# Wave attention: weights by tanh, one per head and two heads later, behind a guard on the amplitudes; VectorE takes the second half of the scores for two heads of four

## The reference, cut to what matters

```
FREQS = [31.0, 37.0, 41.0, 43.0, 47.0]
sim = einsum('bhid,bhjd->bhij', q, k) / sqrt(hd) / (abs(temperature)[0] + 0.1)
scores = zeros_like(sim)
for fi, freq in enumerate(FREQS):
    scores = scores + alpha[h, fi] * sin(2 pi * sim / freq + phi[h, fi])
w = sigmoid(scores)
w = w / (sum(w, axis=-1, keepdims=True) + 1e-10)
out = einsum('bhij,bhjd->bhid', w, v)
```

```
'alpha': jax.random.normal(ks[5], (N_HEADS, len(FREQS)), dtype=jnp.float32) * 0.1
...
factors = {'L0_attn_a_Wq': 8.0, 'L0_attn_a_Wk': 8.0, 'L0_attn_a_Wv': 3.655,
 'L0_attn_a_alpha': 8.0, 'L0_attn_a_phi': 8.0,
...
for name, factor in factors.items():
    out[name] = (out[name] * factor).astype(out[name].dtype)
```

## Time and profile before

| what | value |
|---|---|
| median of 3 runs | 3933.75 us (3931.38 to 3935.47) |
| the profiled execution | 3933.19 us, its span 3931.4 us |
| granted TensorE clock over the span | 0.924 |
| busy share of the span: PE, DVE, ACT, POOL | 81%, 75%, 72%, 24% |
| instructions | 70146 |

### The profile page before, as it was taken

How to read it: one execution, slowest core, us unless ns; L and a number is a source line. 1 busy time by engine, 2 the same in 40 slices (tenths; PEclk the granted TensorE clock), 3 DMA queues, 4 the chain that set the end, 5 groups by cost and what they waited for, 6 DMA issues and landing times. The chain is left out here.

```text
span 3931.4 us, 70146 instructions
## 1 busy us (share of the span) xinstructions
PE 3171.9 (81%) x26580; PEld 1974.0 (50%) x26580; DVE 2951.2 (75%) x4169; ACT 2817.8 (72%) x2401; POOL 925.5 (24%) x983
## 2 busy tenths in 40 slices
PE   4788888888888898898638943798998998998890
PEld 2232233223323332233236941688888888887790
DVE  7788888888888888888565545678787878876562
ACT  3999999999999999999604313576776776774330
POOL 2010111011010101110001442544334435330336
PEclk8899999999999999999868977799999999998995
DMA  5877887788788877877521225412213113112122
GB/s 160 306 295 301 301 330 293 303 311 320 299 306 317 309 300 299 333 293 297 220 71 63 62 54 171 68 27 36 47 20 54 27 27 56 26 18 71 33 61 69
DMA packets 311330, 683.35 MB, mean 174 GB/s; under 512 B 155296, under 2 KB 228608, under 8 KB 310560
## 3 DMA queue, kind: packets, MB, share of 16 engines
q1 hardware_dynamic: 302368, 661.87, 48.6%
q0 software_dynamic: 8704, 17.84, 2.0%
HBM read 90.73 MB, written 52.10 MB: 36 GB/s over the span
## 5 line engine op out<-in xcount | busy, mean ns | idle before, releaser
L740 PE MATMUL psA<-wave,diag 128*128 128x512 f32 x2560 | 1174.2, 606 | 117.3 <-DVE score L879 75.0
L801 ACT ACTIVATE wave<-wave 128x2048 f32<-128x2048 int32 x640 | 1184.8, 1904 | 45.6 <-DMA wave<-score 41.5
L740 PEld LDWEIGHTS psA<-wave,diag 128*128 128x128 f32 x2560 | 468.4, 191 | 727.5 <-issue 594.4
L879 DVE SCALAR_TENSOR_TENSOR score<-wave,par,psA 128x1024 f32<-128x1024 f32 x256 | 316.3, 1278 | 290.2 <-PE psA L740 290.2
L678 POOL TENSOR_TENSOR diag<-ident,par 128x128 f32<-128x128 f32 x384 | 142.5, 399 | 1493.5 <-PE psA L740 1493.3
L851 DVE TENSOR_SCALAR score<-s,par 128x2048 int32<-128x2048 int32 x384 | 482.1, 1285 | 9.2 <-DMA wave<-score 6.1
L879 DVE SCALAR_TENSOR_TENSOR score<-wave,par,score 128x1024 f32<-128x1024 f32 x384 | 470.3, 1282 | 0.0
L1785 POOL COPY kb<-ks 48x1024 bf16<-48x1024 bf16 x160 | 320.9, 2005 | 567.3 <-PE psR L1845 380.6
L716 PE MATMUL psO<-score,Vg 128*9 128x512 f32 x1056 | 284.6, 689 | 105.0 <-ACT score L781 105.0
L1935 ACT ACTIVATE W<-psR 128x1024 f32<-128x1024 f32 x256 | 249.4, 1023 | 133.3 <-PE psR L1870 133.2
L1926 ACT COPY r<-psR 128x1024 f32<-128x1024 f32 x256 | 248.6, 1021 | 103.9 <-PE psR L1845 103.9
(11 more groups left out here) (262 smaller groups left out, 4798.0 us busy)
## 6 DMA issues: line engine op xcount, KB each, us to landing
wave<-score SPq DMA_DIRECT2D x384, 1023.9 KB, 6.3
wave<-s SPq DMA_DIRECT2D x128, 1023.9 KB, 5.2
ks<-kb_parts SPq DMA_DIRECT2D x56, 384.0 KB, 6.2
qs<-qb_parts SPq DMA_DIRECT2D x32, 384.0 KB, 6.2
ys<-f_ys SPq DMA_DIRECT2D x36, 256.0 KB
wave_out<-og SPq DMA_DIRECT2D x33, 256.0 KB, 8.2
o<-wave_out SPq DMA_DIRECT2D x8, 1024.0 KB, 5.3
qp<-qa_parts SPq DMA_DIRECT2D x32, 192.0 KB, 7.2
```

What stands on the lines that cost most here:

```text
L740: mm = pe.matmul(psA[:, kt, :], diag[:, h % 2, f, :], wave[:, h % 2, f, kt * L:(kt + 1) * L], start=(f == 0), stop=(f == PE_F - 1 or (h in ...
L801: act.activation(wave[:, h % 2, f, :], angle[:, h % 2, f, :], ACT.Sin, scale=float(TWO_PI / 2.0 ** 32)).then_inc(sine, 1)
L879: return dve.scalar_tensor_tensor(out=score[:, u * HG + h, cols], in0=wave[:, h % 2, f, cols], scalar=par[:, u, 1, h * NF + f:h * NF + f + ...
```

## The change

1. **Guard.** `far` was 1 where `bound` reached FAR x 31 / 8. Now VectorE takes the maximum of `bound` scaled by 8 / (120 x 31) and of all squared amplitudes, and `far` is 1 where that maximum is at least NEAR = 1.0.
2. **Weights.** In the plain branch Tanh takes Sigmoid's place: sigmoid(s) is 0.5 + 0.5 tanh(s / 2). The missing 0.5 times the sum of the values is added when `psO` is taken out: TensorE sums the values over the keys (`psV`, a matmul with one column), VectorE halves that (`half_v`), ScalarE uses it as a bias. Each head's weights are made behind the sines of the head two later (`weigh`), not four heads at once. The general branch keeps Sigmoid, but also one head at a time.
3. **Scores.** For heads 0 and 2 of each group VectorE takes out the second half (`take_scores` on VectorE, between the angles of head n+1 and the sums of head n).
4. GpSimd clears `Vg`, whose rows are now 32 wide for a head; one Silu of one column is the first activation of the block.

The diff, cut to its core:

```diff
+EVAC_HEADS = (0, 2)
+NEAR = 1.0
...
             def values(g, slot, heads):
                 if heads[0] == 0:
                     pe.wait_ge(v_ready, g + 1)
+                    pe.wait_ge(half_ready, g + C_HALF)
+                    for kt in range(QT):
+                        mm = pe.matmul(psV[:], Vg[:, slot ^ 1, kt, :, :].rearrange("p h d -> p (h d)"),
+                                       Vg[:, slot ^ 1, kt, 0, HD:VW], start=(kt == 0), stop=(kt == QT - 1))
+                    mm.then_inc(v_summed, 1)
...
-            def sigmoids(g, slot):
-                for h in range(HG):
-                    act.wait_ge(added, g * HG * ADDS - (HG - 1 - h) * ADDS + C_ADDED)
-                    act.activation(score[:, slot * HG + h, :], score[:, slot * HG + h, :], ACT.Sigmoid)\
-                       .then_inc(weighed, 1)
+            def weigh(m, at, general):
+                act.wait_ge(added, (m + 1) * ADDS + C_ADDED)
+                if general:
+                    act.activation(score[:, at, :], score[:, at, :], ACT.Sigmoid).then_inc(weighed, 1)
+                else:
+                    act.activation(score[:, at, :], score[:, at, :], ACT.Tanh, scale=0.5).then_inc(weighed, 1)
...
                             if f in (2, NF - 1) and more:
                                 tu, th, tg = (u, h + 2, g) if h < HG - 2 else (1 - u, h + 2 - HG, g + 1)
-                                take_scores(n + 2, tu, th, tg, f // 4, general)
-                        if h == 0:
-                            sigmoids(g, 1 - u)
+                                if f == 2 or th not in EVAC_HEADS:
+                                    take_scores(n + 2, tu, th, tg, f // 4, general)
+                        weigh(n - 2, (u * HG + h - 2) % AR, general)
...
+            act.activation(og[:, 0:1], params[:, 0, 0, 0:1], ACT.Silu)
             act.wait_ge(far_ready, 1)
             with act.If(act.value_load(far[0:1, 0:1])):
                 all_heads(True)
...
                         if not final:
                             make_angles(n + 1, nu, nh, ng, general)
+                        tu, th, tg = (u, h + 2, g) if h < HG - 2 else (1 - u, h + 2 - HG, g + 1)
+                        if th in EVAC_HEADS and not (last and u == 1 and h >= HG - 2):
+                            take_scores(n + 2, tu, th, tg, general)
                         add_sines(n, u, h, g)
-
-
-            dve.tensor_scalar(far[:], bound[:], FAR * min(FREQS) / HD, None, ALU.is_ge).then_inc(far_ready, 1)
+                        if h == 2:
+                            halve_values(g, u)
+
+            amps = params[:, :, 1, :]
+            dve.tensor_scalar(reach[:, 0:1], bound[:], HD / (FAR * min(FREQS)), None, ALU.mult).then_inc(reached, 1)
+            dve.tensor_tensor(reach[:, 1:].rearrange("p (a n) -> p a n", a=GPB), amps, amps, ALU.mult
+                              ).then_inc(reached, 1)
+            dve.wait_ge(reached, 2)
+            dve.tensor_reduce(top_reach[:], reach[:], AX.X, ALU.max).then_inc(reached, 1)
+            dve.wait_ge(reached, 3)
+            dve.tensor_scalar(far[:], top_reach[:], NEAR, None, ALU.is_ge).then_inc(far_ready, 1)
```

More of the change, by code:

```diff
@@ L572, in wave_attention @@
         og = sb(c, "og", [P, L])
-        Vg = sb(c, "Vg", [P, 2, QT, HG, VW])
+        Vg = sb(c, "Vg", [P, 2, QT, HG, P // HG])
+        half_v = sb(c, "half_v", [P, 2])
+        reach = sb(c, "reach", [P, 1 + GPB * HG * NF])
+        top_reach = sb(c, "top_reach", [P, 1])
         psS = ps(c, "psS", [P, 2, L])
@@ L576, in wave_attention @@
         psO = ps(c, "psO", [P, L])
+        psV = ps(c, "psV", [P, 1])
         qk_loaded = [sem(c, f"qk_loaded{i}") for i in range(2)]
@@ L776, in take_scores, with outputs @@
                                    scale=float(2 ** FRAC) / FREQS[0]).then_inc(s_ready, 1)
-            def sigmoids(g, slot):
-                for h in range(HG):
-                    act.wait_ge(added, g * HG * ADDS - (HG - 1 - h) * ADDS + C_ADDED)
-                    act.activation(score[:, slot * HG + h, :], score[:, slot * HG + h, :], ACT.Sigmoid)\
-                       .then_inc(weighed, 1)
-            def outputs(g):
+            def weigh(m, at, general):
[4 more added lines that the diff above has]
+                    act.activation(score[:, at, :], score[:, at, :], ACT.Tanh, scale=0.5).then_inc(weighed, 1)
+            def outputs(g, slot, general):
                 act.wait_ge(valued, 2 * g + 2 + C_VALUED)
                 act.wait_ge(out_stored, g * 16 + C_STORED)
-                act.copy(og[:], psO[:]).then_inc(out_taken, 1)
+                if general:
+                    act.copy(og[:], psO[:]).then_inc(out_taken, 1)
+                else:
+                    act.wait_ge(half_ready, g + 1 + C_HALF)
+                    act.activation(og[:], psO[:], ACT.Identity, bias=half_v[:, 1 - slot:2 - slot],
+                                   scale=0.5).then_inc(out_taken, 1)
             def pair(gg, last, general):
@@ L804, in pair @@
                                 tu, th, tg = (u, h + 2, g) if h < HG - 2 else (1 - u, h + 2 - HG, g + 1)
-                                take_scores(n + 2, tu, th, tg, f // 4, general)
-                        if h == 0:
-                            sigmoids(g, 1 - u)
+                                if f == 2 or th not in EVAC_HEADS:
+                                    take_scores(n + 2, tu, th, tg, f // 4, general)
+                        weigh(n - 2, (u * HG + h - 2) % AR, general)
                         if h == HG - 1:
-                            outputs(g)
+                            outputs(g, 1 - u, general)
             def all_heads(general):
                 for h in range(2):
-                    for half in range(2):
-                        take_scores(h, 0, h, 0, half, general)
+                    take_scores(h, 0, h, 0, 0, general)
+                    if h not in EVAC_HEADS:
+                        take_scores(h, 0, h, 0, 1, general)
                 act.wait_ge(cleared, 2)
@@ L818, in all_heads @@
                 pair(NG // 2 - 1, True, general)
-                sigmoids(NG, 1)
-                outputs(NG)
+                for h in (HG - 2, HG - 1):
+                    weigh((NG - 1) * HG + h, HG + h, general)
+                outputs(NG, 1, general)
+            act.activation(og[:, 0:1], params[:, 0, 0, 0:1], ACT.Silu)
             act.wait_ge(far_ready, 1)
@@ L852, in make_turns, with take_scores @@
                                   ALU.mult, ALU.add).then_inc(done, 1)
+            def take_scores(n, u, h, ng, general):
+                cols = slice(HALF, 2 * HALF)
+                dve.wait_ge(s_ps, n * 2 + 2 + C_SPS)
+                if not (isinstance(n, int) and n < 2):
+                    dve.wait_ge(carried[0][h % 2], (ng * (HG // 2) + h // 2) * 16)
+                if general:
+                    dve.tensor_copy(s[:, h % SR, cols], psS[:].rearrange("p a n -> p (a n)")).then_inc(s_ready, 1)
+                else:
+                    dve.wait_ge(par_ready, ng + 1)
+                    dve.tensor_scalar(first[:, h % SR, cols], psS[:].rearrange("p a n -> p (a n)"),
+                                      float(2 ** FRAC) / FREQS[0], par[:, u, 0, h * NF:h * NF + 1],
+                                      ALU.mult, ALU.add).then_inc(s_ready, 1)
             def make_angles(n, u, h, gn, general):
@@ L936, in all_heads @@
                 pair(NG // 2 - 1, True, general)
+                halve_values(NG, 0)
             with dve.If(dve.value_load(far[0:1, 0:1])):
```

27 lines of the change are left out of this document (21 added, 6 removed).

## The result

The changed kernel takes 7365.12 us (median; 7359.96 to 7366.48) against 3932.57 for the kernel before beside it: a ratio of 1.873, 95% interval 1.870 to 1.876. The forecast was 7,355. The profiled execution took 7366.48 us, the longest of the four.

What follows compares the result with a forecast made beforehand. ScalarE bounds the old heads; in the general branch VectorE's angles and the copy wait do. 137.3 us, 127 periods of 40.9 (5194) and 29.5 put the last store at 5361, +3421 on 3933.2: 7,355 us, range 6,960 to 7,610.

Steps and rivals of the forecast that it cites:

- The branch: Guard before the heads: largest amplitude 2.196, square 4.82, exceeds 1.0, so VectorE and ScalarE take the general branch for all heads.
- A frequency: VectorE's angles in the general branch: four dependent instructions of 2048 columns, 6.045 us per frequency, 30.3 us for five.
- The wait for the burst: VectorE's next angles wait for the copy of frequency 2, 10.6 us behind the first issue; idle 3.5 or 2.3 us.
- What was costed at nothing: General branch heads: ScalarE's table loads (246 us in all), VectorE's score halves (0.6 us per head) and TensorE's work lie covered.
- Rival 2: Heads, general branch: the burst of copies doesn't hold up VectorE; period 37.9 us, 381 us less, 6,974 us; chance 10%.
- The sum: Heads: angles of head 0 end at 137.3 us, 127 periods take 5194, last head 29.5; last store at 5361, +3421 us.
- tail: Last head, from its first copy to the last store: copies, sines, table load, sigmoids, values and psO's copy, 29.5 us.
- 1, the plain branch: Heads: the guard stays under 1 and the plain branch runs; 142 us less, 3,790 us; chance 6%.
- the further loads of the general branch: ScalarE in the heads: table loads rise from 2 in four heads to 2 a head, 246 us in all, beside VectorE.
- 3, two-scalar instructions at one column per cycle: VectorE's first two angle instructions cost 2.29 us each; +1,363 us, 8,718 us; chance 4%.
- the two terms of the period: One head's step in the general branch: 10.6 us from first copy issue to next angles, plus 30.3 us of angles, 40.9 us.

## Why the prediction was right

- **The branch.** The step that decides it, the inputs' amplitudes against the new guard (largest 2.196, square 4.82), held: 640 of each general instruction, and the guard alone turns 7365 into 3765.
- **A frequency.** 6.045 us were forecast. The angles' stretch of five took 30.64, not 30.3; without GpSimd beside it 30.35. The instruction durations were within 0.01 us, but for those into `wave` that GpSimd lengthened (1.315 and 1.257 for 1.225).
- **The wait for the burst.** Forecast 10.6 us from first issue to the next angles, measured 10.35; VectorE's idle time per head 2.75 us, forecast 3.5 or 2.3. With the copies earlier it went altogether, and the time with it. Its parts aren't quite those of the forecast: 58.7 of the 349 us are the loop's gaps, in the place of a shorter wait.
- **What was costed at nothing.** Table loads, VectorE's halves of the scores, `psV` and its halving: the old kernel's general branch runs at 40.87 us per head against 41.00. That cover is real; with the wait gone the halves cost 1.1 us each. Rival 2 said so.
- **The sum.** Start of the last pieces: first copy 136.5 (137.3 forecast), 127 x 41.0 = 5207 (5194), tail 31.8 (29.5). The errors are -0.8, +13 and +2.3 us, together 14; what follows the heads took 2 us less, and the median lies 1.4 us under the profiled execution, not 0.6 over it, so the whole came out 10 us over the forecast of 7,355. Part of this closeness is luck: the angles were 0.34 us per head too cheap (43 us in all) and the wait 0.25 us too long (32 us), and the two nearly cancel.
- **The rivals.** 1, the plain branch, has been run: 3765, not 3,790, and it wasn't the case; its sum took 64 table loads where the earlier trace rows have 80. The same count makes the further loads of the general branch 226 us and not 246, which changed nothing, since they are covered. 2, no wait for the burst, isn't what the kernel does. With the order changed it can be had: 38.43 us per head against the 37.9 of its price, the difference being GpSimd's 0.3 us and 31.4 / 127 = 0.25 us of loop gaps. 3, two-scalar instructions at one column per cycle, fell: 1.22 us each.
- **What was missed** is small: GpSimd's 0.3 us per head, taken at 0; the gap at the jump back, not thought of; and in the tail the last head's values, 5.30 us (granted clock 0.72) where 3.6 were taken from a stretch at 1.00.

## What to carry to other kernels

A guard that picks one of two versions of a loop is a part of the change like any other: compute what it yields for the inputs that are timed before costing a single instruction, since here it was worth 3,600 us and the rest 170. A branch that the trace doesn't show can still be priced closely (here within 0.2%, part of it luck; the two terms of the period by themselves within 1.2 and 2.4%), if each instruction is matched with the nearest row of its form, dependent neighbours are counted apart from independent ones, and the moment at which its transfers start is followed to who waits for them. Where a branch is meant to be slow but rare, the order in which a queue takes its copies is worth a look: one line gave back 4%.

## What was not expected of the hardware

- GpSimd's 128x128 multiplications took 1.62 us beside VectorE's single-source and two-source instructions in the general branch, 0.40 beside its sums in the plain one, and lengthened VectorE's by 0.3 us per head.
- At each jump back of its loop in the general branch VectorE idled 4.1 to 4.5 us on average (14 times with 8 heads in the body, 4 with 24), and 2.2 us with early copies; the waits of the kernel before show none.
- Where ScalarE had no wait, a table load cost its 1.283 us and nothing visible besides.
- TensorE, 36% busy in the heads, was granted 0.66 of its clock there, and 0.90 to 0.99 when 86 to 94% busy. It cost at least 1.7 us, in the last head's values; VectorE waited for TensorE only once in the heads, 10.6 us in the last.
